# A ring of 41 slots in place of two halves of 20, and the rounds of a block behind the whole next product

## The chip, the cores and the metric

One core of a Trainium2 chip runs the kernel. The metric is the device time of one execution in microseconds, the median of three runs.

## The reference

Two graph layers with a residual and a layer norm each, on x (5120 x 64) with a dense stored adjacency matrix adj (5120 x 5120, float32, 105 MB). The first, cut to what matters:

```
e = concat(c_u * (diag_u * x_u @ W_u) + x_u,  c_i * (diag_i * x_i @ W_i) + x_i)
h = adj @ (adj.T @ e)
x = layernorm(x + layernorm(h) * gamma + beta + x)
```

The second layer drops edges by a softmax threshold. The kernel takes the largest row sum of squares of adj while it reads it; where that stays under a bound, no edge can survive, the message is zero, and the output is layernorm(x), which the first layer's last step can give at once. With these inputs it is so; the branches for surviving edges (`message_pe` and the others) are built and not taken.

## The kernel before, in words

adj is read once, in 10 blocks of 512 columns. A block is 40 tiles of 128 rows (`T` = 40), and two tiles are a unit: 128 x 1024 float32, 512 KB, one load into one slot of 4 KB a partition (`SLOT` = 1024). There are 200 units. `slot_of(v)` puts even blocks into slots 20 to 39 and odd blocks into 0 to 19 (`SLOT_FIRST`, line 44).

For each block c there are two products. The first, adj_c.T @ e, takes the units as they come (`multiply_unit`, matmul on line 1455, 8 TensorE instructions a unit) and sums all 20 in one PSUM bank (`block_bank`). VectorE turns the finished sum in 32 x 32 squares (`turn_half`, 1268), and ScalarE and GpSimd spread it over `col_sum` (`keep_cols`, 1157 and 1079), which has two buffers, for even and odd blocks. The second product, adj_c @ that sum, needs the units transposed: VectorE turns each unit in its slot (`turn_unit`, 1259) once TensorE has used it and ScalarE has scanned it. It runs in rounds of 10, 14 and 16 tiles (`PARTS`, line 47), each in one half of PSUM (`round_banks`, four banks, lower or upper by `upper_banks`), with 128 TensorE instructions a round whatever its size (`multiply_round`, 1475). VectorE adds each round to `h_sum` (`add_round`, 1279, and 1277 for block 0).

A slot is free for the unit two blocks later when the round that reads it is done: SyncE, which issues all loads in order of units (1028), waits for `round_done` of that round (1027). ScalarE scans each unit as it lands (`scan`, 1144 to 1149: squares into one of two scratch tiles, with an accumulator read), waiting for the scan two before, which used the same scratch.

The order of TensorE is written out by hand (1516 to 1541). Block 0's rounds lie between the units of block 1 and the first two of block 2 (`AHEAD`). From then on, with c from 1 to 8: 16 units of block c + 1, round 0 of block c, 4 units of block c + 1, rounds 1 and 2 of block c. At the end block 9's first two rounds (12 and 12 tiles) come before the last round of block 8, and the norm's steps (`close_tiles`, 1490) lie between the rest. VectorE has an order to match (1293 to 1328, then 1367 on).

Slots that are not yet or no longer in use hold other things: x, its transposed pairs and the small weights before block 1 is loaded (so SyncE waits for `e_made`, 1023), x once more at the end (`X_SLOT`, 126, in slots of block 8). `center_t` and `center_g` are small tiles for gamma, used once by the matmul on line 1523.

Of the kernel before, what the change touches and what calls it, by code (L numbers as in the profile page):

```python
# [7 lines left out]
def adjacency_layers_kernel(nc, x, adj, w_ui, scales, gamma, beta,  # L8
# [13 lines left out]
    P = 128  # L22
# [20 lines left out]
    SLOTS = 40  # L43
    SLOT_FIRST = [20 if c % 2 == 0 else 0 for c in range(NB)]
    assert sum(WIDTHS) == N and max(WIDTHS) == CH

    PARTS = [((0, 10), (10, 14), (24, 16))] * (NB - 1)
    PARTS += [((0, 12), (12, 12), (24, 8), (32, 8))]

# [9 lines left out]

    AHEAD = 2  # L60
# [37 lines left out]
    with ctx:  # L98
# [27 lines left out]
        X_SLOT = 20  # L126
# [21 lines left out]
        scratch = [sb(f"scratch{k}", [P, SLOT], bf16) for k in range(2)]  # L148
# [3 lines left out]
        center_t = sb("center_t", [D, P])  # L152
        center_g = sb("center_g", [D, D])
# [7 lines left out]
        inv_d = sb("inv_d", [P, TPG])  # L161
        neg_inv_d = sb("neg_inv_d", [P, TPG])
        eps_tile = sb("eps_tile", [P, TPG])


        piece_at = [N * i for i in range(4)] + [ln_at + N * i for i in range(4)]
        piece = [pooled[:, a:a + N] for a in piece_at]
        assert 4 * N <= x_at and piece_at[-1] + N <= POOLED
# [33 lines left out]
        diagonal = carve(P)  # L202
        node_a, node_b, node_c = carve(T), carve(T), carve(T)
# [151 lines left out]
        def slot_of(v):  # L355
            c, i = place_of_unit(v)
            return SLOT_FIRST[c] + i

# [7 lines left out]
        def banks_of_block(c):  # L366

            return c % 2 == 0

        def upper_banks(g):  # L370

            c = place_of_round(g)[0]
            if c == NB - 1:
                return banks_of_block(NB - 2) == (g != LAST)
            return banks_of_block(c) == (c == NB - 2 or g < ROUNDS_AT[c + 1] - 1)
# [32 lines left out]
        def turned_of(g):  # L410

            c, first, nt = place_of_round(g)
            w = WIDTHS[c]
            at = SLOT * SLOT_FIRST[c] + w * first
            return pooled[:, at:at + w * nt].rearrange("p (t b r) -> p t b r", b=w // 32, t=nt)
# [577 lines left out]
        def message_pool(pool):  # L993
# [10 lines left out]
            pool.wait_ge(gate, (ROUNDS * STAGES + 1) * SHARERS)  # L1004
            with pool.Fori(0, GROUPS) as g:
                step = Steps(pool, g * STEPS1)
                layer_norm(pool, step, ln_h, g * SUMS1, ln_out, (g + 1) * 16)
# [4 lines left out]
        def _(sp):  # L1012
            for k in range(LGROUPS):
                sp.dma_start(x_first[:, group_tiles(k), :], tile_rows(x, GT * k, GT)).then_inc(x_loaded[k], 16)  # L1014
            for v in range(UNITS):
                c, i = place_of_unit(v)
                ut, c0 = UNIT_TILES[c], COL_FIRST[c]
                if v == UNIT_FIRST[1]:
                    sp.dma_start(gamma_sb[:, :], gamma).then_inc(norm_in, 16)  # L1019
                    sp.dma_start(beta_sb[:, :], beta.partition_broadcast(P)).then_inc(norm_in, 16)  # L1020

                    assert SLOT_FIRST[1] == 0 and SETUP_SLOTS <= UPB[1]
                    sp.wait_ge(e_made, LGROUPS)
# [28 lines left out]
        def _(pool):  # L1052
            for tile, value in ((ident, 0.0), (center, 0.0), (minus_half, -0.5), (inv_d, 1.0 / D),
                                (neg_inv_d, -1.0 / D), (eps_tile, LN_EPS)):
                nc.gpsimd.memset(tile[:, :], value).then_inc(cleared, 1)
            pool.wait_ge(cleared, 6)
# [79 lines left out]
        def _(act):  # L1136
# [7 lines left out]
            def scan(v):  # L1144
                wait_loaded(act, v)
                if v >= 2:
                    act.wait_ge(unit_scanned, v - 1)
                nc.scalar.activation(scratch[v % 2][:, :], slots[slot_of(v)], ACT.Square,  # L1148
                                     accum_out=square_sum[:, v:v + 1]).then_inc(unit_scanned, 1)
# [67 lines left out]
        def _(dve):  # L1217
# [92 lines left out]
            for v in range(UNIT_FIRST[1] + 18, UNIT_FIRST[2] + AHEAD):  # L1310
                turn_unit(v)
            add_round(2)


            for c in range(1, NB - 1):
                first = UNIT_FIRST[c + 1]
                for v in range(first + AHEAD if c == 1 else first, first + 13):
                    turn_unit(v)
                add_round(ROUNDS_AT[c])
                turn_unit(first + 13)  # L1320
                turn_half(c + 1)
                if c == NB - 2:
                    break
                for v in range(first + 14, first + 19):
                    turn_unit(v)
                add_round(ROUNDS_AT[c] + 1)
                turn_unit(first + 19)
                add_round(ROUNDS_AT[c] + 2)

# [90 lines left out]
        def _(pe):  # L1420
# [21 lines left out]
            def multiply_unit(v):  # L1442
# [4 lines left out]
                if i == 0 and c >= 2:  # L1447
                    pe.wait_ge(halves_turned_b, c - 1)
                    same = before_in_banks(ROUNDS_AT[c - 1], banks_of_block(c))
                    pe.wait_ge(round_added, same[-1] + 1)  # L1450
# [8 lines left out]
            def multiply_round(g):  # L1459
# [7 lines left out]
                pe.wait_ge(halves_turned_b, c + 1 if banks_of_block(c) == upper_banks(g) else min(c + 2, NB))  # L1467
                if g == 2:
                    pe.wait_ge(center_kept, 1)
# [54 lines left out]
            for v in range(UNIT_FIRST[1] + 12, UNIT_FIRST[2] + AHEAD):  # L1524
# [3 lines left out]


            for c in range(1, NB - 1):  # L1530
                first = UNIT_FIRST[c + 1]
                for v in range(first + AHEAD if c == 1 else first, first + 16):
                    multiply_unit(v)
                multiply_round(ROUNDS_AT[c])
                for v in range(first + 16, first + 20):
                    multiply_unit(v)
                multiply_round(ROUNDS_AT[c] + 1)
                if c < NB - 2:
                    multiply_round(ROUNDS_AT[c] + 2)
# [52 lines left out]
```

## Time and profile before

| | us |
|---|---|
| median of 3 runs (lowest, highest) | 398.53 (398.12, 398.65) |
| the profiled execution | 398.46 |
| its span, first to last instruction | 396.70 |
| TensorE busy in it | 379.2 (96%) |
| VectorE, ScalarE, GpSimd busy | 317.0, 267.5, 63.9 |
| read from HBM | 107.60 MB |

Times in views are from the start of the span. A row of a timeline gives the start, the busy time of the instructions merged in it, the engine and line, what is written from what, how many, and in brackets the idle time just before with what ended it. TensorE's instructions overlap, and their ends are modelled, so a row's length can reach a little over the start of the next.

### The profile page before, as it was taken

What the parts mean: (1) busy time and instruction counts of PE and PEld (TensorE: products, weight loads), DVE (VectorE), ACT (ScalarE), POOL (GpSimd) and SP (SyncE); (2) the same over time, 40 slices, a digit from 0 to 9 for tenths busy, and PEclk for the clock granted to TensorE, in tenths of its full rate; (3) what the DMA queues carried; (4) which work ended last, traced back from release to release, by engine and by line L of the source; (5) the groups of instructions that cost most, each with busy time, mean ns of one, the idle gap of its engine ahead of it and who ended that gap; (6) DMA issues with size and microseconds to landing.
All of it is one profiled execution on the core that took longest, in us unless ns stands there. A gap on an engine that the chain in (4) does not pass through costs nothing.

```text
span 396.7 us, 13295 instructions
## 1 busy us (share of the span) xinstructions
PE 379.2 (96%) x5762; PEld 220.4 (56%) x5762; DVE 317.0 (80%) x306; ACT 267.5 (67%) x515; POOL 63.9 (16%) x125
## 2 busy tenths in 40 slices
PE   8987999999999999999999999999999999999980
PEld 7743556465456546545654664565466456555770
DVE  1699799797788869787976979697698869795674
ACT  2596995996878577587857768685876868501133
POOL 2000300300200300030030003003000300276375
PEclk9999999999999999999999999999999999999996
DMA  8999999894798789579877967996895799300012
GB/s 286 389 387 380 386 386 387 314 388 156 267 377 296 268 311 386 198 268 391 310 264 252 388 222 270 393 339 204 311 387 192 270 393 368 141 3 2 24 35 85
DMA packets 56991, 109.83 MB, mean 277 GB/s; under 512 B 3808, under 2 KB 4576, under 8 KB 56928
## 3 DMA queue, kind: packets, MB, share of 16 engines
q1 hardware_dynamic: 56640, 108.84, 75.9%
q8 instruction: 47, 0.77, 0.8%
q10 hardware_dynamic: 288, 0.09, 0.1%
q14 instruction: 16, 0.13, 0.1%
HBM read 107.60 MB, written 1.31 MB: 275 GB/s over the span
## 4 chain that ended last, share of the span: by engine, by line
PE 85%; SPq 8%; DMA 3%; DVE 1%; POOL 1%; issue 1%; POOLq 0%; ACT 0%; DVEq 0%
PE quad L1475 44%; PE quad L1455 39%; SPq L1028 6%; DMA pooled<-in_adj 3%; PE quad L1490 2%; SPq L1019 1%; DVE pooled L1279 1%; POOL pooled L1107 1%; SPq L1014 1%; POOLq L98 0%; POOL pooled L1102 0%; DVE pooled L1346 0%; DVE pooled L1355 0%; SPq L1020 0%; DVE pooled L1332 0%
## 5 line engine op out<-in xcount | busy, mean ns | idle before, releaser
L1259 DVE STREAM_TRANSPOSE pooled<-pooled 128x1024 f32<-128x1024 f32 x200 | 229.8, 1208 | 7.9 <-ACT scratch L1148 7.9
L1148 ACT ACTIVATE scratch<-pooled 128x1024 bf16<-128x1024 f32 x200 | 210.0, 1051 | 36.1 <-DMA pooled<-in_adj 34.5
L1455 PE MATMUL quad<-pooled,rows_in 128*64 128x256 f32 x1600 | 180.7, 381 | 4.0 <-DMA pooled<-in_adj 4.0
L1475 PE MATMUL quad<-pooled,col_sum 32*64 32x320 f32 (+4 forms) x3968 | 177.5, 507 | 0.6 <-issue 0.2
L1455 PEld LDWEIGHTS quad<-pooled,rows_in 128*64 128x64 f32 x1600 | 111.8, 137 | 74.5 <-issue 12.5
L1475 PEld LDWEIGHTS quad<-pooled,col_sum 32*64 32x64 f32 x3968 | 88.1, 132 | 82.7 <-issue 63.7
L1279 DVE TENSOR_TENSOR pooled<-pooled,quad 128x1280 f32<-128x1280 f32 (+5 forms) x29 | 52.4, 1808 | 43.4 <-PE quad L1475 43.3
L1079 POOL COPY col_sum<-col_half 32x256 f32<-32x256 f32 x80 | 31.6, 394 | 312.4 <-DVE col_half L1268 309.5
L1157 ACT COPY col_sum<-col_half 32x256 f32<-32x256 f32 x80 | 32.3, 403 | 42.5 <-DVE col_half L1268 41.7
L1148 ACT ACTIVATION_READ_ACCUMULATOR scratch<-pooled 128x1 f32 x200 | 37.4, 187 | 0.0
L1178 ACT ACTIVATE pooled<-quad 128x256 f32<-128x256 f32 (+2 forms) x7 | 3.3, 476 | 25.2 <-PE quad L1490 25.2
L1490 PE MATMUL quad<-center,pooled 128*128 128x128 f32 x80 | 10.2, 281 | 1.6 <-DVE pooled L1279 0.9
L1490 PEld LDWEIGHTS quad<-center,pooled 128*128 128x128 f32 x80 | 9.3, 191 | 4.0 <-issue 2.7
L1268 DVE STREAM_TRANSPOSE col_half<-quad 128x256 f32<-128x256 f32 x10 | 4.4, 441 | 7.2 <-PE quad L1455 7.2
L1107 POOL TENSOR_TENSOR pooled<-pooled,minus_half 128x4 f32<-128x4 f32 (+2 forms) x7 | 8.9, 1277 | 7.5 <-DVE pooled L1355 7.4
L1186 ACT ACTIVATE pooled<-pooled 128x256 f32<-128x256 f32 (+2 forms) x7 | 3.5, 507 | 9.6 <-DVE pooled L1350 7.7
L1102 POOL TENSOR_TENSOR pooled<-pooled,minus_half 128x4 f32<-128x4 f32 (+2 forms) x7 | 8.9, 1282 | 4.7 <-DVE pooled L1332 4.6
L1142 ACT COPY pooled<-quad 128x512 f32<-128x512 f32 x5 | 2.8, 587 | 9.8 <-PE quad L1428 9.8
L1232 DVE TENSOR_TENSOR rows_in<-quad,pooled 128x256 f32<-128x256 f32 x10 | 3.7, 411 | 3.6 <-PE quad L1438 3.4
L1097 POOL TENSOR_TENSOR pooled<-pooled,beta_sb 128x512 f32<-128x512 f32 x5 | 6.4, 1277 | 0.4
L1277 DVE COPY pooled<-quad 128x1280 f32<-128x1280 f32 (+2 forms) x3 | 5.8, 1922 | 0.8 <-PE quad L1475 0.8
L1438 PE MATMUL quad<-pooled 64*128 64x64 f32 x80 | 5.5, 278 | 0.3 <-ACT pooled L1142 0.3
(48 smaller groups left out, 60.1 us busy)
## 6 DMA issues: line engine op xcount, KB each, us to landing
pooled<-in_adj SPq DMA_DIRECT2D x200, 512.0 KB, 9.2
pooled<-in_x SPq DMA_DIRECT2D x5, 256.0 KB, 3.7
pooled<-in_x SPq DMA_DIRECT2D x1, 768.0 KB, 5.1
pooled<-in_x SPq DMA_DIRECT2D x1, 512.0 KB, 3.5
out<-pooled SPq DMA_DIRECT2D x2, 256.0 KB, 2.5
out<-pooled SPq DMA_DIRECT2D x2, 192.0 KB, 3.0
out<-pooled SPq DMA_DIRECT2D x3, 128.0 KB, 2.0
pooled<-in_w_ui ACTq DMA_DIRECT2D x1, 64.0 KB, 3.3
```

Of the source, the lines that this page charges most:

```text
L1028: sp.dma_start(slots[slot_of(v)].rearrange("p (t k) -> p t k", t=ut), tile_rows(adj, ut * i, ut)[:, :, c0:c0 + WIDTHS[c]]).then_inc(unit_l ...
L1079: kept = nc.gpsimd.tensor_copy(spread_to(c, a, 1, f), spread_from(c, 1, f))
L1097: nc.gpsimd.tensor_tensor(xk, xk, beta_sb[:, :].unsqueeze(1).to_broadcast([P, GT, D]), ALU.add).then_inc(x_steps, 1)
L1102: nc.gpsimd.tensor_tensor(rstd[:, norm_tiles(k)], var[:, norm_tiles(k)], minus_half[:, 0:norm_size(k)], ALU.pow).then_inc(rstd_made, 1)
L1107: nc.gpsimd.tensor_tensor(scale[:, norm_tiles(k)], y_var[:, norm_tiles(k)], minus_half[:, 0:norm_size(k)], ALU.pow).then_inc(scale_made, 1)
L1148: nc.scalar.activation(scratch[v % 2][:, :], slots[slot_of(v)], ACT.Square, accum_out=square_sum[:, v:v + 1]).then_inc(unit_scanned, 1)
L1157: kept = act.copy(spread_to(c, a, 0, f), spread_from(c, 0, f))
L1259: nc.vector.transpose(tiles, tiles).then_inc(unit_turned, 1)
L1279: nc.vector.tensor_tensor(to, to, share, ALU.add).then_inc(round_added, 1)
L1455: mm = pe.matmul(block_bank(c)[half(h), 0:w // 2], rows_in[:, t, :], slots[slot_of(v)][:, at:at + w // 2], start=(t == 0), stop=(t == T - 1))
L1475: mm = pe.matmul(round_banks(g)[a][half(b % 2), 0:w].rearrange("p (t r) -> p t r", r=32), col_sum[c % 2][quadrant(a), b, :], to[quadrant(a ...
L1490: mm = pe.matmul(nat_of(k)[:, i, :], h_sum[:, P * (first + i):P * (first + i) + P], center[:, :], start=True, stop=True)
```

## The change

The two halves become one ring of 41 slots: unit v of the whole sequence sits in slot (9 + v) mod 41, so a unit takes the slot of the unit before it two blocks earlier. Three blocks get other sizes of rounds, so that no round crosses the ring's end (blocks 3, 5 and 7 with first rounds of 10, 12 and 14 tiles). For the blocks 1 to 7 TensorE does all 20 units of the next block and then the three rounds in a row; VectorE's order follows. The first products of all blocks but 0 use the lower banks; the rounds of a block use upper, lower, upper, and those of blocks 0 and 8 only upper ones. ScalarE's two scratch tiles become one, so a scan waits for the scan just before it, `center_t` and `center_g` move into `h_sum` (VectorE waits for `gamma_turned` before round 2 of block 0 is added), and three constants move into the part for surviving edges. The diff, cut to its core:

```diff
@@ -40,12 +40,17 @@
-    SLOTS = 40
-    SLOT_FIRST = [20 if c % 2 == 0 else 0 for c in range(NB)]
+    SLOTS = 41
+    SLOT_FIRST = [(9 + UNIT_FIRST[c]) % SLOTS for c in range(NB)]
...
     PARTS = [((0, 10), (10, 14), (24, 16))] * (NB - 1)
+    PARTS[3] = ((0, 10), (10, 16), (26, 14))
+    PARTS[5] = ((0, 12), (12, 16), (28, 12))
+    PARTS[7] = ((0, 14), (14, 16), (30, 10))
     PARTS += [((0, 12), (12, 12), (24, 8), (32, 8))]
...
-    AHEAD = 2
...
-        X_SLOT = 20
+        X_SLOT = 5
...
-        scratch = [sb(f"scratch{k}", [P, SLOT], bf16) for k in range(2)]
+        scratch = sb("scratch", [P, SLOT], bf16)
...
-        center_t = sb("center_t", [D, P])
-        center_g = sb("center_g", [D, D])
+
+        center_t = h_sum[0:D, N - P:N]
+        center_g = h_sum[0:D, N - P - D:N - P]
...
-            return SLOT_FIRST[c] + i
+            return (SLOT_FIRST[c] + i) % SLOTS
...
-            return c % 2 == 0
+            return c == 0
 
         def upper_banks(g):
...
             c = place_of_round(g)[0]
-            if c == NB - 1:
-                return banks_of_block(NB - 2) == (g != LAST)
-            return banks_of_block(c) == (c == NB - 2 or g < ROUNDS_AT[c + 1] - 1)
+            if c in (0, NB - 2):
+                return True
+            return g != (LAST if c == NB - 1 else ROUNDS_AT[c] + 1)
...
-
-                    assert SLOT_FIRST[1] == 0 and SETUP_SLOTS <= UPB[1]
+                if v < UNIT_FIRST[2] and slot_of(v) == 0:
+
+                    assert c == 1 and i + SETUP_SLOTS <= UPB[1]
                     sp.wait_ge(e_made, LGROUPS)
...
-            for tile, value in ((ident, 0.0), (center, 0.0), (minus_half, -0.5), (inv_d, 1.0 / D),
-                                (neg_inv_d, -1.0 / D), (eps_tile, LN_EPS)):
+            for tile, value in ((ident, 0.0), (center, 0.0), (minus_half, -0.5)):
                 nc.gpsimd.memset(tile[:, :], value).then_inc(cleared, 1)
-            pool.wait_ge(cleared, 6)
+            pool.wait_ge(cleared, 3)
...
-                if v >= 2:
-                    act.wait_ge(unit_scanned, v - 1)
-                nc.scalar.activation(scratch[v % 2][:, :], slots[slot_of(v)], ACT.Square,
+                if v:
+                    act.wait_ge(unit_scanned, v)
+                nc.scalar.activation(scratch[:, :], slots[slot_of(v)], ACT.Square,
                                      accum_out=square_sum[:, v:v + 1]).then_inc(unit_scanned, 1)
...
-            for v in range(UNIT_FIRST[1] + 18, UNIT_FIRST[2] + AHEAD):
+            for v in range(UNIT_FIRST[1] + 18, UNIT_FIRST[2]):
                 turn_unit(v)
+            dve.wait_ge(gamma_turned, 1)
             add_round(2)
 
 
-            for c in range(1, NB - 1):
+            for c in range(1, NB - 2):
                 first = UNIT_FIRST[c + 1]
-                for v in range(first + AHEAD if c == 1 else first, first + 13):
+                for v in range(first, first + 14):
+                    turn_unit(v)
+                turn_half(c + 1)
+                for v in range(first + 14, first + 18):
                     turn_unit(v)
                 add_round(ROUNDS_AT[c])
-                turn_unit(first + 13)
-                turn_half(c + 1)
-                if c == NB - 2:
-                    break
-                for v in range(first + 14, first + 19):
+                for v in range(first + 18, first + 20):
                     turn_unit(v)
                 add_round(ROUNDS_AT[c] + 1)
-                turn_unit(first + 19)
                 add_round(ROUNDS_AT[c] + 2)
+
+
+            for v in range(UNIT_FIRST[NB - 1], UNITS - 7):
+                turn_unit(v)
+            add_round(ROUNDS_AT[NB - 2])
+            turn_unit(UNITS - 7)
+            turn_half(NB - 1)
...
                 if i == 0 and c >= 2:
-                    pe.wait_ge(halves_turned_b, c - 1)
+
+                    pe.wait_ge(halves_turned_b, c)
                     same = before_in_banks(ROUNDS_AT[c - 1], banks_of_block(c))
-                    pe.wait_ge(round_added, same[-1] + 1)
+                    if same:
+                        pe.wait_ge(round_added, same[-1] + 1)
...
-                pe.wait_ge(halves_turned_b, c + 1 if banks_of_block(c) == upper_banks(g) else min(c + 2, NB))
-                if g == 2:
+                pe.wait_ge(halves_turned_b, 1 if upper_banks(g) else min(c + 2, NB))
+                if g == ROUNDS_AT[1] + 1:
                     pe.wait_ge(center_kept, 1)
...
-            for v in range(UNIT_FIRST[1] + 12, UNIT_FIRST[2] + AHEAD):
+            for v in range(UNIT_FIRST[1] + 12, UNIT_FIRST[2]):
                 multiply_unit(v)
             multiply_round(2)
 
 
-
-            for c in range(1, NB - 1):
-                first = UNIT_FIRST[c + 1]
-                for v in range(first + AHEAD if c == 1 else first, first + 16):
+            for c in range(1, NB - 2):
+                for v in range(UNIT_FIRST[c + 1], UNIT_FIRST[c + 2]):
                     multiply_unit(v)
-                multiply_round(ROUNDS_AT[c])
-                for v in range(first + 16, first + 20):
-                    multiply_unit(v)
-                multiply_round(ROUNDS_AT[c] + 1)
-                if c < NB - 2:
-                    multiply_round(ROUNDS_AT[c] + 2)
+                for g in range(ROUNDS_AT[c], ROUNDS_AT[c + 1]):
+                    multiply_round(g)
+
+
+            for v in range(UNIT_FIRST[NB - 1], UNITS - 4):
+                multiply_unit(v)
+            multiply_round(ROUNDS_AT[NB - 2])
+            for v in range(UNITS - 4, UNITS):
+                multiply_unit(v)
+            multiply_round(ROUNDS_AT[NB - 2] + 1)
             multiply_round(LAST)
             multiply_round(LAST + 1)
             close_tiles(0)
```

## Rows read from the trace of the kernel before

**Rows 1.** the page: busy time by engine, and the chain by engine

```profile
PE 379.2 (96%) x5762; PEld 220.4 (56%) x5762; DVE 317.0 (80%) x306; ACT 267.5 (67%) x515; POOL 63.9 (16%) x125
...
PE 85%; SPq 8%; DMA 3%; DVE 1%; POOL 1%; issue 1%; POOLq 0%; ACT 0%; DVEq 0%
```

**Rows 2.** timeline of TensorE: start us, busy us, instruction

```profile
42.83 1.08 PE L1455 MATMUL quad<-pooled,rows_in 128*64 128x256 f32 x8 [0.27 <-DMA pooled<-in_adj]
...
61.27 8.85 PE L1455 MATMUL quad<-pooled,rows_in 128*64 128x256 f32 x80
...
70.33 7.13 PE L1475 MATMUL quad<-pooled,col_sum 32*64 32x512 f32 x128 [0.20 <-issue]
...
110.79 14.03 PE L1455 MATMUL quad<-pooled,rows_in 128*64 128x256 f32 x128
...
124.75 4.56 PE L1475 MATMUL quad<-pooled,col_sum 32*64 32x320 f32 x128
...
129.24 3.67 PE L1455 MATMUL quad<-pooled,rows_in 128*64 128x256 f32 x32
...
132.85 13.13 PE L1475 MATMUL quad<-pooled,col_sum 32*64 32x448 f32 x256
...
145.91 14.03 PE L1455 MATMUL quad<-pooled,rows_in 128*64 128x256 f32 x128
...
343.61 16.59 PE L1475 MATMUL quad<-pooled,col_sum 32*64 32x448 f32 x384
...
371.86 3.71 PE L1475 MATMUL quad<-pooled,col_sum 32*64 32x256 f32 x128
```

**Rows 3.** timeline of SyncE's queue, loads of line 1028

```profile
129.41 0.37 SPq L1028 DMA_DIRECT2D pooled<-in_adj  x1
...
139.22 0.37 SPq L1028 DMA_DIRECT2D pooled<-in_adj  x1
...
314.85 0.37 SPq L1028 DMA_DIRECT2D pooled<-in_adj  x1
```

**Rows 4.** timeline of ScalarE, scans that waited for their load

```profile
143.03 1.06 ACT L1148 ACTIVATE scratch<-pooled 128x1024 bf16<-128x1024 f32 x1 [0.94 <-DMA pooled<-in_adj]
...
161.87 1.06 ACT L1148 ACTIVATE scratch<-pooled 128x1024 bf16<-128x1024 f32 x1 [0.16 <-DMA pooled<-in_adj]
...
337.57 1.06 ACT L1148 ACTIVATE scratch<-pooled 128x1024 bf16<-128x1024 f32 x1 [0.15 <-DMA pooled<-in_adj]
```

**Rows 5.** stretches: busy us (count) by engine, granted clock, DMA share, GB/s

```profile
135.00:136.00 1.00, 1.00 (x32) 0.45 (x24) 1.00 (x2) 0.96 (x4) 0.92 (x3) 1.00 0.94 291
...
141.50:160.50 19.00, 19.00 (x238) 11.14 (x229) 15.31 (x13) 14.39 (x26) 0.00 (x0) 1.00 1.05 389
...
273.00:276.00 3.00, 3.00 (x60) 1.30 (x64) 2.53 (x3) 2.00 (x5) 1.85 (x5) 1.00 0.90 281
```

**Rows 6.** timelines of ScalarE, GpSimd and VectorE in the first 53 us

```profile
16.53 1.06 ACT L1148 ACTIVATE scratch<-pooled 128x1024 bf16<-128x1024 f32 x1
...
17.49 0.19 ACT L1148 ACTIVATION_READ_ACCUMULATOR scratch<-pooled 128x1 f32 x1
...
17.58 1.04 ACT L1148 ACTIVATE scratch<-pooled 128x1024 bf16<-128x1024 f32 x1
...
40.21 3.31 ACT L1157 COPY col_sum<-col_half 32x256 f32<-32x256 f32 x8 [3.13 <-DVE col_half L1268]
...
1.48 0.29 POOL L1057 TENSOR_SCALAR_AFFINE_SELECT ident<-ident 128x128 f32<-128x128 f32 x1 [0.25 <-POOL eps_tile L1055]
...
52.23 0.15 DVE L1248 TENSOR_SCALAR beta_sum<-beta_sum 128x1 f32<-128x1 f32 x1
...
52.42 0.26 DVE L1250 TENSOR_SCALAR beta_sb<-beta_sb,beta_sum 128x64 f32<-128x64 f32 x1
```

**Rows 7.** timeline of VectorE in the block from 145.91

```profile
146.09 2.29 DVE L1279 TENSOR_TENSOR pooled<-pooled,quad 128x2048 f32<-128x2048 f32 x1 [3.69 <-PE quad L1475]
...
148.29 14.76 DVE L1259 STREAM_TRANSPOSE pooled<-pooled 128x1024 f32<-128x1024 f32 x13
```

More of the change, by code:

```diff
@@ L41, in adjacency_layers_kernel @@
     UNITS = UNIT_FIRST[NB]
-    SLOTS = 40
-    SLOT_FIRST = [20 if c % 2 == 0 else 0 for c in range(NB)]
+    SLOTS = 41
+    SLOT_FIRST = [(9 + UNIT_FIRST[c]) % SLOTS for c in range(NB)]
     assert sum(WIDTHS) == N and max(WIDTHS) == CH
     PARTS = [((0, 10), (10, 14), (24, 16))] * (NB - 1)
+    PARTS[3] = ((0, 10), (10, 16), (26, 14))
+    PARTS[5] = ((0, 12), (12, 16), (28, 12))
+    PARTS[7] = ((0, 14), (14, 16), (30, 10))
     PARTS += [((0, 12), (12, 12), (24, 8), (32, 8))]
+    assert all((SLOT_FIRST[c] + t // UNIT_TILES[c]) % SLOTS + nt // UNIT_TILES[c] <= SLOTS
+               for c in range(NB) for t, nt in PARTS[c])
     ORDER = [(c,) + part for c in range(NB - 1) for part in PARTS[c]]
@@ L160, in adjacency_layers_kernel @@
         minus_half = sb("minus_half", [P, GT])
[L161 to L166, printed above, removed]
+        piece_at = [0] + [ln_at + N * i for i in range(7)]
         piece = [pooled[:, a:a + N] for a in piece_at]
-        assert 4 * N <= x_at and piece_at[-1] + N <= POOLED
+        assert N <= x_at and piece_at[-1] + N <= POOLED
         ring, turned, carved_from, rest = piece[0:4], piece[4:6], piece[6], piece[7]
@@ L202, in adjacency_layers_kernel @@
         diagonal = carve(P)
+        inv_d, neg_inv_d, eps_tile = carve(TPG), carve(TPG), carve(TPG)
         node_a, node_b, node_c = carve(T), carve(T), carve(T)
@@ L413, in turned_of @@
             w = WIDTHS[c]
-            at = SLOT * SLOT_FIRST[c] + w * first
+            at = SLOT * slot_of(UNIT_FIRST[c] + first // UNIT_TILES[c])
             return pooled[:, at:at + w * nt].rearrange("p (t b r) -> p t b r", b=w // 32, t=nt)
@@ L1004, in message_pool @@
             pool.wait_ge(gate, (ROUNDS * STAGES + 1) * SHARERS)
+            for tile, value in ((inv_d, 1.0 / D), (neg_inv_d, -1.0 / D), (eps_tile, LN_EPS)):
+                nc.gpsimd.memset(tile[:, :], value).then_inc(cleared, 1)
+            pool.wait_ge(cleared, 6)
             with pool.Fori(0, GROUPS) as g:
```

## Prediction

> **What bounds the kernel now.** Read first the page's engine line and its chain. TensorE is busy 96% of the span, and 85% of the chain that ended last is TensorE; transfers hold 3% of it, nearly all in the first 43 us [rows 1]. From 43 to 360 us TensorE is the clock of everything, so the next view is its timeline [rows 2]. One block costs 35.12 us (from 110.79 to 145.91), and it is made of four runs: 16 units of the next first product, round 0, the last 4 units, rounds 1 and 2. The starts follow each other without a gap. So this change can only gain by what TensorE loses when it goes from one kind of work to the other, and can only lose by making TensorE wait.
>
> The switch has a price that the rows give. Unit runs take 8.85 us for 80 instructions and 14.03 for 128: 0.108 us each (0.863 for a unit of 8) and 0.22 once per run. Round runs take 4.56 us for 10 tiles and 13.13 for two rounds with 30 tiles: 0.4285 a tile and 0.27 once. The run of three rounds, 38 tiles, takes 16.59, where 0.4285 x 38 + 0.27 = 16.55: the constant belongs to the run, not to the round. The 8-tile round fits too (3.70 against 3.71). The next run starts 0.07 before the modelled end of the last, so a run costs 0.15 (units) or 0.20 (rounds). Check: 20 x 0.863 + 40 x 0.4285 + 2 x 0.15 + 2 x 0.20 = 35.10, read 35.12 [rows 2].
>
> **What is removed.** In the blocks 1 to 7 the rounds now form one run behind one run of 20 units: 0.35 us less in each of 7 cycles, 2.45. The split of the 40 tiles among three rounds moves, their sum doesn't. Round 2 of block 0 waited 0.20 us for the turned half of block 1, as it shared its banks [rows 2]; it now goes to the upper banks, where nothing is late: 0.20. In all 2.65 us less, if the data are there. Block 0 and the end (16 units, round 0 of block 8, 4 units, the rest) keep their order and are costed at nothing.
>
> **What is moved: the time in which slots come free.** Unit i of a block is loaded into the slot of unit i - 1 two blocks before. Before, round 0 ran in the middle of the next product, and 15 of the 20 loads were let go by rounds 1 and 2. After, unit 0 goes into the spare slot, but units 1 to 19 all wait for round 0, which now starts only when the whole product between is done. The loop of the changed kernel is then: round 0, release, 19 loads, last unit, round 0. I compute both sides from the release.
>
> TensorE's side: SyncE issues 4.66 us after a 10-tile round started (129.41 against 124.75) [rows 2, 3]. The three rounds take 17.14 + 0.20 = 17.34, so the product starts 12.68 after the issue and its unit 19 is wanted 19 x 0.863 = 16.40 later: 29.1 us after the issue.
>
> The loads' side: ScalarE scans each unit as it lands, so its starts that end a wait on DMA are landings. In the stretch that follows the issue at 139.22, the first of 15 units lands at 143.03 (3.81 later), the 14th, the last but one, at 161.87 (22.65 later) [rows 3, 4]. The last such stretch gives 337.57 - 314.85 = 22.72, and the four between lie from 22.5 to 23.05. The queues move 389 GB/s there [rows 5], 1.35 us for a unit of 524,288 bytes; 13 steps would be 17.55, and 18.84 are read, so somewhere 1.29 us are lost in each stretch while the bytes flow at an even rate. After the change unit 19 is the last but one of 20 loads (unit 0 of the next block follows it): 22.7 + 5 x 1.35 = 29.45 us. It comes 0.35 us late, and the restart makes the last unit 1.08 instead of some 0.96 us (42.83 alone, as in the start [rows 2]): 0.45 us a cycle. The cover that hid the loads, 4 us of round 0 in the middle of the product, is gone.
>
> The rule on completion in the Trainium skill (DMA: Bandwidth & Descriptors, section "Why a DMA increments its semaphore by 16 and not by 1") says that a transfer counts as landed only when the slowest of its engines is done; by that, one engine that falls behind delays every later unit though the rate looks whole. The even 389 GB/s beside the lost 1.29 us agrees.
>
> Cycle by cycle: block 2's loads start early enough (slots of block 0 are free by 76 us), no stall. Blocks 3, 4, 5, 6 and 8: 0.45 each, 2.25. Block 7 waits for round 0 of block 5, which now has 12 tiles, so the release is 0.86 later: 1.3. Block 9 waits for a 14-tile round 0 (1.71 later), but its last 4 units run after a round; its unit 15 lands 24.05 after the issue and is wanted 23.9 after it: 0.15. Sum 3.7 us.
>
> One more cost is due to lost slack. The rate sags now and then: 291 GB/s in 135 to 136, 281 in 273 to 276 [rows 5], 0.25 + 0.83 = 1.1 us of transfer lost in the stretches behind round 0, where nobody waited then. Six of seven such stretches now end on the path: 0.9 us (bounds 0 and 2).
>
> **What is hidden.** VectorE: 20 transposes at 1.135 us are 22.7 us of a block, and three round sums are under 2.3 each [rows 7], so some 5 us are free. In the new order 14 transposes end 0.9 us after the product, the half is turned by 1.4, and the lower banks are wanted by round 1 at 4.5; if that cover went, TensorE would wait for the difference. Every unit is turned a whole product before its round. The 8 copies of col_sum on ScalarE and GpSimd (3.3 us) are wanted 17 us later. SyncE: the wait for e_made moves 12 loads down its queue; it is over by then in any case (TensorE can't have used block 0 without e), and the gamma and beta loads stay where they were. GpSimd has three memsets less to wait for before ident, but TensorE is then in its warm-up: 0. The wait for gamma_turned on VectorE holds back add_round(2) alone, which comes 10 us later.
>
> ScalarE's single scratch adds a wait of each scan for the scan before. Now a scan starts every 1.04 us, even 0.10 before the accumulator read of the last ends (17.49 + 0.19 = 17.68, next at 17.58) [rows 6]. No row shows ScalarE waiting for itself. VectorE does it in 0.04 us (0.15 us from 52.23, next at 52.42), GpSimd in 0.25 (idle before 1.48) [rows 6]: 1.19 to 1.40 us a scan. [...] It matters in one place, the start: 19 scans from 16.53 must end before the copies at 40.21, which a spacing up to 1.25 allows; at 1.40 round 0 of block 0 would start up to 2.3 us late. Later ScalarE follows the loads at 1.35 a unit and has time. Cost 0, bounds 0 and 2.3.
>
> **The sum.** The profiled execution took 398.46 us (span 396.70 and 1.76 around it), 0.07 under the median of 398.53. 398.46 - 2.65 + 3.7 + 0.9 = 400.4.
>
> **Rivals.** (1) The loads arrive in time: faster. If the 1.29 us don't recur in a stretch begun by round 0, unit 19 lands 28.15 after the issue, before 29.1, block 7 is just met, and 2.65 remain: 395.8. For it: the loss is not seen in every step, and the stretches behind round 0 can't be read (ScalarE is busy copying). Against: it is there in all six stretches (the first and the last of them: [rows 3, 4]). It decides where a landing is under 29.1. The Trainium skill (same page, section "Anatomy of one DMA", a fit for GpSimd's queue) gives 2.0 us plus bytes over 436 GB/s. An estimate by it puts the 19 units at 24.8 us, that is, on the side of this rival at 395.8; the 389 GB/s and the 3.81 us to the first landing speak against both of its figures here. (2) A draw: the lateness is there, but 0.1 to 0.3 a cycle, and gives back what the runs gained: 397.7 to 399.3, likeliest 398.6. (3) The loss grows with the length of the stretch: 1.29 x 18/13 = 1.79, 0.5 more in 7 cycles: 403.9. (4) The single scratch is slow at the start, 1.30 or more a scan: 1 to 2.3 us on top, around 402, or 397 with rival 1. (5) A run of merged rounds doesn't lose its constants, since the banks change between them: then 2.45 is not gained; against it speaks the 38-tile run [rows 2].
>
> **Chances.** The forecast (stalls of 0.35 us a cycle or more, to 402) 0.45; rival 1 0.28; rival 2 0.15; rivals 3 to 5 together 0.12. What a measurement of this kernel can tell from no change is about 0.2%, 0.8 us. Faster than 397.7: 0.30 (rival 1 and the edge of 2). Within: 0.15. Slower than 399.3: 0.55. The range must reach to rival 1, as it holds more than 2 in 10: 395.7 below, and 402.8 above, which leaves out most of rival 3. The forecast alone would have 399.3 to 402.
>
> **What the next profile would show.** In TensorE's timeline runs of 160 unit instructions, each ahead of one run of 384 round instructions. Right: a block takes about 35.2 us, not 34.8; the unit run is cut near its end by a wait on the loads; that wait is longest in block 7, at 36; DMA idles some 4 us a block, all of it ahead of round 0's end; round 2 of block 0 has no wait. Wrong: unit runs of 17.5 us with no wait on DMA (rival 1), scans further apart than 1.25 us in the first 40 us (rival 4), or 0.2 us between rounds of one run (rival 5). The forecast stands or falls with one number, the landing of unit 19 after the issue behind round 0: each 0.1 us of it moves the sum by 0.7.

## The result and the profile after

| | before | after |
|---|---|---|
| median of 6 runs (lowest, highest) | 398.54 us (397.60, 399.28) | 401.94 us (400.82, 402.55) |
| ratio, with its 95% interval | | 1.008 (1.0064 to 1.0096) |
| profiled execution, its span | 398.46, 396.70 | 400.82, 399.0 |

The change costs 3.4 us in the medians. The page of the changed kernel, busy time by engine and the chain by engine, to hold against [rows 1]:

```profile
PE 378.5 (95%) x5762; PEld 218.8 (55%) x5762; DVE 316.2 (79%) x306; ACT 276.2 (69%) x515; POOL 63.8 (16%) x122
...
PE 64%; DMA 17%; SPq 14%; DVE 1%; issue 1%; POOL 1%; POOLq 0%; ACT 0%; DVEq 0%
```

TensorE is busy for the same time, but the chain has moved: TensorE's share fell from 85% to 64%, transfers rose from 3% to 17% and SyncE's queue from 8% to 14%. The loads have come onto the path. TensorE's timeline shows where (start us, busy us, instruction, how many, idle before with what ended it); the lines from 60.48 on answer to [rows 2]:

```profile
60.48 7.13 PE L1468 MATMUL quad<-pooled,rows_in 128*64 128x256 f32 x64
67.53 7.12 PE L1488 MATMUL quad<-pooled,col_sum 32*64 32x512 f32 x128
...
109.38 15.81 PE L1468 MATMUL quad<-pooled,rows_in 128*64 128x256 f32 x144
125.56 1.08 PE L1468 MATMUL quad<-pooled,rows_in 128*64 128x256 f32 x8 [0.38 <-DMA pooled<-in_adj]
126.84 1.08 PE L1468 MATMUL quad<-pooled,rows_in 128*64 128x256 f32 x8 [0.20 <-DMA pooled<-in_adj]
127.86 17.44 PE L1488 MATMUL quad<-pooled,col_sum 32*64 32x320 f32 x384
145.23 17.69 PE L1468 MATMUL quad<-pooled,rows_in 128*64 128x256 f32 x160
162.85 17.44 PE L1488 MATMUL quad<-pooled,col_sum 32*64 32x320 f32 x384
...
197.30 1.08 PE L1468 MATMUL quad<-pooled,rows_in 128*64 128x256 f32 x8 [0.21 <-DMA pooled<-in_adj]
...
233.47 17.80 PE L1488 MATMUL quad<-pooled,col_sum 32*64 32x384 f32 x384
251.21 14.96 PE L1468 MATMUL quad<-pooled,rows_in 128*64 128x256 f32 x136
266.43 1.08 PE L1468 MATMUL quad<-pooled,rows_in 128*64 128x256 f32 x8 [0.27 <-DMA pooled<-in_adj]
268.88 1.08 PE L1468 MATMUL quad<-pooled,rows_in 128*64 128x256 f32 x8 [1.37 <-DMA pooled<-in_adj]
270.17 1.08 PE L1468 MATMUL quad<-pooled,rows_in 128*64 128x256 f32 x8 [0.21 <-DMA pooled<-in_adj]
271.19 17.44 PE L1488 MATMUL quad<-pooled,col_sum 32*64 32x320 f32 x384
```

The new order is there: 160 unit instructions, 384 round instructions, with no constant lost between rounds of a run (17.44 us for 40 tiles; 0.4285 x 40 + 0.27 = 17.41). One run of rounds, from 233.47, took 17.80; the 0.36 us more are no wait on a load. Round 2 of block 0 (67.53) has lost its wait of 0.20. But unit runs end in single units of 8 instructions, each behind a wait on a load, as at the start of the kernel. Where no wait is printed, as in 145.23, the run is still longer (17.69) than the 17.49 that it takes with data at hand.

The stretches from one first product to the next answer to the 35.12 us between 110.79 and 145.91 in [rows 2] (columns: stretch, its length, busy us and count of TensorE, weight loads, VectorE, ScalarE, GpSimd, granted clock, DMA share, GB/s):

```profile
109.38:145.23 35.85, 35.28 (x553) 19.59 (x545) 28.71 (x24) 27.06 (x50) 3.16 (x8) 1.00 0.83 302
145.23:180.22 34.99, 34.99 (x552) 19.74 (x544) 28.86 (x24) 26.29 (x50) 3.16 (x8) 1.00 0.83 298
180.22:215.69 35.47, 35.24 (x553) 19.67 (x545) 28.45 (x24) 25.90 (x48) 3.16 (x8) 1.00 0.83 301
215.69:251.21 35.52, 35.37 (x553) 19.88 (x545) 29.24 (x24) 25.35 (x48) 3.16 (x8) 1.00 0.79 284
251.21:288.56 37.35, 35.51 (x546) 19.48 (x544) 28.18 (x24) 27.11 (x51) 3.15 (x8) 1.00 0.82 297
288.56:323.68 35.12, 35.01 (x552) 19.75 (x544) 29.51 (x24) 24.95 (x47) 3.15 (x8) 1.00 0.78 282
```

The granted clock is 1.00 (the 2.4 GHz level) and the work the same in each of the six, yet they take 35.0 to 37.35 us.

This profiled execution is the fastest of the six. From the unit run behind gamma (60.48, before 61.27) to the 38-tile run (345.78, before 343.61) it took 2.96 us more; the part ahead of it, where the first loads set the pace, was 0.79 shorter, and what follows 0.13 longer.

### The profile page after: what moved, and what is told of

It is laid out like the page before. It is cut to its first block, busy times and chain, and to the rows that moved or that the text cites. A ratio compares the mean times of both kernels' runs of the same rounds, so it can differ in the third digit from the quotient of the medians.

```text
span 399.0 us, 13294 instructions
## 1 busy us (share of the span) xinstructions
PE 378.5 (95%) x5762; PEld 218.8 (55%) x5762; DVE 316.2 (79%) x306; ACT 276.2 (69%) x515; POOL 63.8 (16%) x122
## 4 chain that ended last, share of the span: by engine, by line
PE 64%; DMA 17%; SPq 14%; DVE 1%; issue 1%; POOL 1%; POOLq 0%; ACT 0%; DVEq 0%
PE quad L1488 44%; PE quad L1468 18%; DMA pooled<-in_adj 17%; SPq L1034 13%; PE quad L1503 2%; SPq L1024 1%; DVE pooled L1284 1%; POOL pooled L1112 1%; SPq L1019 1%; POOLq L101 0%; POOL pooled L1107 0%; DVE pooled L1357 0%; DVE pooled L1366 0%; SPq L1025 0%; DVE pooled L1343 0%
## 5 line engine op out<-in xcount | busy, mean ns | idle before, releaser
L1488 PE MATMUL quad<-pooled,col_sum 32*64 32x512 f32 (+4 forms) x3968 | 176.1, 506 | 0.3 <-DVE pooled L1284 0.2
L1284 DVE TENSOR_TENSOR pooled<-pooled,quad 128x2048 f32<-128x2048 f32 (+5 forms) x29 | 52.2, 1802 | 50.6 <-PE quad L1488 50.5
```

The lines of the kernel that those rows point to most:

```text
L1284: nc.vector.tensor_tensor(to, to, share, ALU.add).then_inc(round_added, 1)
L1488: mm = pe.matmul(round_banks(g)[a][half(b % 2), 0:w].rearrange("p (t r) -> p t r", r=32), col_sum[c % 2][quadrant(a), b, :], to[quadrant(a ...
```

## Experiments

The theory: TensorE gains 2.65 us, and all the loss is loads that are late because 19 of 20 wait for a round 0 that starts only behind the whole product. Rivals: the scratch, the ring with its other sizes of rounds, or the merged runs themselves cost time.

**One scratch alone.**

```diff
-        scratch = [sb(f"scratch{k}", [P, SLOT], bf16) for k in range(2)]
+        scratch = sb("scratch", [P, SLOT], bf16)
...
-                if v >= 2:
-                    act.wait_ge(unit_scanned, v - 1)
+                if v:
+                    act.wait_ge(unit_scanned, v)
```

> The kernel before with one part of the change alone: ScalarE's two scratch tiles become one, so a scan waits for the scan just before it. Theory (late loads): scans stand 1.24 us apart where they followed each other at 1.04, nobody waits for them, and the time stays at 398.5 us (398.2 to 398.9). Rival (the single scratch is part of the loss): 399.3 to 402. In this kernel VectorE turns a unit sooner after its scan than in the changed one, so this is the harder case for the scratch.

Measured 398.74 us, ratio 1.0004 (0.999 to 1.0019). The scans of its trace (ScalarE, around the copies of col_sum) stand 1.24 us apart; [rows 6] had 1.04:

```profile
37.80 1.06 ACT L1148 ACTIVATE scratch<-pooled 128x1024 bf16<-128x1024 f32 x1
...
39.04 1.06 ACT L1148 ACTIVATE scratch<-pooled 128x1024 bf16<-128x1024 f32 x1
...
40.17 3.31 ACT L1157 COPY col_sum<-col_half 32x256 f32<-32x256 f32 x8
```

The last scan before the copies ends just in time for them (they start at 40.17; 40.21 before). So the scratch costs nothing, by a small margin: beyond 1.25 us a scan it would have held up round 0 of block 0, by the prediction's count.

**Loads that can't be late, in either order.**

```diff
+                lt = 1 if c in FEW else ut
-                sp.dma_start(slots[slot_of(v)].rearrange("p (t k) -> p t k", t=ut),
-                             tile_rows(adj, ut * i, ut)[:, :, c0:c0 + WIDTHS[c]]).then_inc(...)
+                sp.dma_start(slots[slot_of(v)].rearrange("p (t k) -> p t k", t=ut)[:, 0:lt, :],
+                             tile_rows(adj, ut * i, lt)[:, :, c0:c0 + WIDTHS[c]]).then_inc(...)
```

with `FEW = range(3, NB)`, put into the kernel before:

> The kernel before, but from block 3 on only the first tile of each unit is loaded (256 KB in place of 512 KB; the second tile keeps what was in the slot). Part of the computation is left out: the output isn't the reference's. Everything else, with all waits, stays. Loads were hidden already from 43 us on, so every theory expects 398.5 us (398.0 to 398.8); it is the partner of the next kernel.

and into the changed one:

> The changed kernel with the same half loads from block 3 on (part of the computation is left out, the output isn't the reference's). No load can be late. Theory (TensorE gains 0.35 us for each pair of runs merged and 0.2 at round 2 of block 0, and all the loss is late loads): 2.65 us under the kernel before, 395.9 (395.4 to 396.4), TensorE without a gap in any unit run. Rival (the new order doesn't gain, or the scratch or the banks cost): 398 or more.

Measured 398.58 us (0.9997, 0.9985 to 1.0009) and 395.46 us (0.9917, 0.99 to 0.9934). TensorE's timeline of the second:

```profile
60.76 7.13 PE L1470 MATMUL quad<-pooled,rows_in 128*64 128x256 f32 x64
...
109.66 17.49 PE L1470 MATMUL quad<-pooled,rows_in 128*64 128x256 f32 x160
127.07 17.44 PE L1490 MATMUL quad<-pooled,col_sum 32*64 32x320 f32 x384
144.45 17.49 PE L1470 MATMUL quad<-pooled,rows_in 128*64 128x256 f32 x160
...
340.46 16.59 PE L1490 MATMUL quad<-pooled,col_sum 32*64 32x448 f32 x384
```

Every cycle takes 34.79 us, 0.33 less than 35.12, and from 60.76 to 340.46 it is 279.70 where the kernel before had 282.34: 2.64 less. So the order brings what the runs' constants promised, and the loss of the changed kernel is gone with half of its load traffic. The further 0.4 lies ahead of 60 us, where the kept profiles of all kernels differ by a microsecond in any case (the run behind gamma starts between 60.48 and 61.59).

**The order undone, the ring kept.** In blocks 1 to 7 round 0 stands behind 16 units again (`SPLIT = range(1, 8)`), with banks and VectorE's order to match:

```diff
+                if c in SPLIT:
+                    for v in range(UNIT_FIRST[c + 1], UNIT_FIRST[c + 2] - 4):
+                        multiply_unit(v)
+                    multiply_round(ROUNDS_AT[c])
+                    for v in range(UNIT_FIRST[c + 2] - 4, UNIT_FIRST[c + 2]):
+                        multiply_unit(v)
+                    multiply_round(ROUNDS_AT[c] + 1)
+                    multiply_round(ROUNDS_AT[c] + 2)
+                    continue
```

> The changed kernel with the order of work undone: ring of 41 slots, single scratch and the changed sizes of rounds stay, but in all blocks 1 to 7 round 0 stands behind 16 units again. Theory (the order alone makes the loads late; ring, sizes and scratch cost nothing): 398.3 (397.9 to 398.7). Rival (the ring or the other round sizes are part of the loss): 400 or more.

Measured 397.89 us, 0.9989 (0.9979 to 0.9999). The interval lies just under 1: ring, scratch and the sizes of the rounds cost nothing, and together (with the wait of 0.20 us at round 2 of block 0 gone) they bring some 0.4 us. The loss belongs to the order.

**One more load behind the release.** The changed order with the old 40 slots:

```diff
-    SLOTS = 41
-    SLOT_FIRST = [(9 + UNIT_FIRST[c]) % SLOTS for c in range(NB)]
+    SLOTS = 40
+    SLOT_FIRST = [20 if c % 2 == 0 else 0 for c in range(NB)]
```

and without the three lines on `PARTS[3]`, `PARTS[5]` and `PARTS[7]` (the tiles that lie in the slots before and after use move back with it). Beside it the changed kernel once more.

> The changed kernel without the spare slot: 40 slots in two halves as before, rounds of 10, 14 and 16 tiles in every block, the order of work of the changed kernel. Unit 0 of a block now waits for round 0 too, so the last unit is the 20th load behind the release, not the 19th. Theory (late loads): 1.35 us more in each of six cycles, 8.1; block 7's release comes 0.86 earlier than in the changed kernel: 401.9 + 7.2 = 409. Rival (the wait isn't a matter of the number of loads behind the release): 402.

> The changed kernel once more, beside the next ones on the same chip: 401.9 us (400.8 to 402.6), and its own loss of 1 to 3 us in the unit runs of blocks 3 to 8.

Measured 408.67 us (1.0257, 1.0231 to 1.0284) against 402.05 (1.0087, 1.0065 to 1.0108): 6.6 us more, where 7.2 were expected. In its trace the unit runs end in more waits on loads, and one of 1.18 us where a transfer came late:

```profile
110.04 14.17 PE L1465 MATMUL quad<-pooled,rows_in 128*64 128x256 f32 x128
124.49 1.08 PE L1465 MATMUL quad<-pooled,rows_in 128*64 128x256 f32 x8 [0.27 <-DMA pooled<-in_adj]
126.75 1.08 PE L1465 MATMUL quad<-pooled,rows_in 128*64 128x256 f32 x8 [1.18 <-DMA pooled<-in_adj]
128.04 1.08 PE L1465 MATMUL quad<-pooled,rows_in 128*64 128x256 f32 x8 [0.21 <-DMA pooled<-in_adj]
```

**An earlier and a later release.** First the rounds of blocks 1, 2, 4 and 6 with a first round of 8 tiles, then 12 tiles in blocks 1, 2, 3, 4 and 6:

```diff
+    for c in (1, 2, 4, 6):
+        PARTS[c] = ((0, 8), (8, 16), (24, 16))
```

```diff
-    PARTS[3] = ((0, 10), (10, 16), (26, 14))
+    for c in (1, 2, 3, 4, 6):
+        PARTS[c] = ((0, 12), (12, 12), (24, 16)) if c == 1 else ((0, 12), (12, 14), (26, 14))
```

> The changed kernel, but the rounds of blocks 1, 2, 4 and 6 have 8, 16 and 16 tiles in place of 10, 14 and 16, so SyncE is let go 0.86 us earlier in these four; their loads are those of blocks 3, 4, 6 and 8. Theory (the loop is release, 19 loads, last unit): the lateness of these four cycles in the profile of the changed kernel was 1.10, 0.24, 0.77 and 0.37 us over a full-speed cycle; each gets back up to 0.86, in all 2.2 us: 399.7 from 401.9. Rival (the size of the first round doesn't matter): 401.9.

> The changed kernel with first rounds of 12 tiles in blocks 1, 2, 3, 4 and 6 (12, 12, 16 in block 1, else 12, 14, 14), so the release comes 0.86 us later in five cycles. Smaller first rounds (8 tiles) had cost 3 us, with the DMA rate falling to 66 to 86 GB/s for a microsecond behind the first four loads. Theory (each load's place behind the release counts, and the queue must not run dry before the next round is done; six loads last 8.1 us, the next release comes after 6): 5 x 0.86 = 4.3 more than the changed kernel, 406.3 (405.3 to 407). Rival (the stalls come from the queue running dry behind small first rounds, so larger ones cure them): under 402.

Measured 404.98 us (1.0167, 1.0127 to 1.0207) and 404.79 us (1.0155, 1.014 to 1.0171). The first is a miss: 3 us more than the changed kernel, not 2.2 less. Its DMA rate behind an 8-tile round (block 4's, released at 204.2) shows what happened (columns as above, GB/s last):

```profile
203.50:211.00 7.50, 7.50 (x160) 3.36 (x152) 5.33 (x5) 3.57 (x7) 0.87 (x3) 1.00 0.77 263
211.00:212.00 1.00, 1.00 (x24) 0.36 (x16) 0.95 (x1) 0.83 (x3) 0.00 (x0) 1.00 0.43 143
212.00:213.00 1.00, 1.00 (x32) 0.47 (x24) 1.00 (x1) 0.97 (x2) 0.00 (x0) 1.00 0.72 147
218.00:230.00 12.00, 12.00 (x114) 8.02 (x112) 12.00 (x10) 9.51 (x18) 0.00 (x0) 1.00 1.04 386
```

Four loads let go by a round of 8 tiles last 3.81 + 3 x 1.35 = 7.9 us from the issue; the next release comes 16 x 0.4285 = 6.9 us after it, and its bytes need another 1 to 2 us to flow, so the queues run half empty for two microseconds (143 and 147 GB/s). At 386 GB/s the bytes missed in them are 1.25 us of transfer, more than the 0.86 us that the earlier release brought. The changed kernel has a smaller hole of this kind itself: block 3's first round of 10 tiles is followed by one of 16, and behind it the rate falls to 244 and 344 GB/s for two microseconds (175.5 to 177.5). With 12 tiles there is no such hole, and the kernel takes 2.7 us more than the changed one. That is outside the range expected, but far from the rival's 402: a later release costs time, though a cycle's loss isn't the release alone. Of the three first rounds tried, 10 tiles followed by 14 (6.0 us, against 5 loads that last 9.2) is the best.

**Four rounds, the first of 6 tiles.** Blocks 2 to 7 get rounds of 6, 10, 12 and 12 tiles or the like (block 1: 8, 16, 16), with banks that alternate:

```diff
-    PARTS[3] = ((0, 10), (10, 16), (26, 14))
-    PARTS[5] = ((0, 12), (12, 16), (28, 12))
-    PARTS[7] = ((0, 14), (14, 16), (30, 10))
+    PARTS[1] = ((0, 8), (8, 16), (24, 16))
+    for c in (2, 4, 6):
+        PARTS[c] = ((0, 6), (6, 10), (16, 12), (28, 12))
+    PARTS[3] = ((0, 6), (6, 10), (16, 10), (26, 14))
+    PARTS[5] = ((0, 6), (6, 10), (16, 12), (28, 12))
+    PARTS[7] = ((0, 6), (6, 10), (16, 14), (30, 10))
```

> The changed kernel with its stall cured: four rounds in the blocks 2 to 7, the first of 6 tiles (block 1 keeps three, 8, 16 and 16), banks alternating so that the last round never holds up the next product. The release comes 1.71 us earlier than with 10 tiles, 2.57 earlier in block 5, and a further round in one run costs TensorE nothing. Theory: no stall but some 0.3 us in block 3, and the 2.65 us are kept: 396.2 (395.8 to 397), faster than both kernels. Rival (rounds cost TensorE 0.27 us each even in one run, or VectorE's fourth sum comes late): 398 or more.

Measured 413.97 us (1.0386, 1.0364 to 1.0407), a miss by 18 us. The loads are on time, as expected: from block 4 on the unit runs take 17.49 us. It is the round runs that have holes:

```profile
149.75 17.49 PE L1479 MATMUL quad<-pooled,rows_in 128*64 128x256 f32 x160
167.17 9.31 PE L1499 MATMUL quad<-pooled,col_sum 32*64 32x192 f32 x319
177.65 5.42 PE L1499 MATMUL quad<-pooled,col_sum 32*64 32x320 f32 x127 [1.18 <-issue]
184.24 3.91 PE L1499 MATMUL quad<-pooled,col_sum 32*64 32x448 f32 x66 [1.17 <-issue]
```

The idle times end in "issue": TensorE waited for nothing that the profile shows, in the middle of a round, where the code has no wait. The stretch from 145 to 148 in windows (TensorE busy 1.12 of 3 us, the DMA engines full, 399 GB/s):

```profile
145.00:148.00 3.00, 1.12 (x30) 0.56 (x12) 0.00 (x0) 1.27 (x3) 0.00 (x0) 1.00 1.05 399
```

A round takes 128 matmul and 128 weight-load records whatever its size, so a fourth round puts 1,024 records in place of 768 into 17.4 us. Either the instructions came late or VectorE's sums did (VectorE is idle in this stretch, 0.00 us busy, which speaks against the second), and the same kernel with half loads was to tell. Its further edit is the one shown above for half loads.

> The four-round kernel (e_four, 414 us, whose unit runs had no wait but whose round runs had gaps of 0.3 to 2.2 us in mid-round with nothing to wait for), with half loads from block 3 on: only the first tile of each unit is loaded, so part of the computation is left out and the output isn't the reference's. Theory A (TensorE ran out of instructions: 512 matmul and 512 weight-load records in 17.4 us, fetched over DMA engines that are full of loads): with the queues half empty the gaps vanish, 395.5 as in the changed kernel with half loads. Theory B (the instructions can't come faster whatever the loads do, or a wait on VectorE's sums is behind it): the gaps stay, 408 or more.

Measured 396.82 us (0.9948, 0.9936 to 0.9961). Most round runs are whole, two are 0.8 and 0.7 us too long:

```profile
127.69 17.48 PE L1501 MATMUL quad<-pooled,col_sum 32*64 32x192 f32 x512
...
162.52 18.31 PE L1501 MATMUL quad<-pooled,col_sum 32*64 32x192 f32 x512
...
198.18 18.14 PE L1501 MATMUL quad<-pooled,col_sum 32*64 32x192 f32 x512
```

Of 18.5 us over the changed kernel with half loads, 1.4 are left (some 1.7 of the 18.5 were a late load in block 3, whose release comes from an 8-tile round followed by one of 16). VectorE's work and all waits are the same in both, so the holes come from load traffic meeting many TensorE instructions. The Trainium skill (Runtime: NRT & Kernel Launch, section "Instruction fetch mechanics") says that instructions are refilled in blocks of 16 KiB (256 instructions) by the sequencer's own DMA queue, and calls that cost mostly hidden. The traces bear out the blocks: the instruction queue moved 47 packets in the changed kernel and 53 here, six more for six more rounds of 256 records each, and each packet has 16,384 bytes.

That it is the fetch can be read from the four-round kernel's trace. Counted in order, matmuls and weight loads together, its holes stand at TensorE's records 4033, 5058, 5313, 6338, 6593, 9154, 9409 and 10689, always a multiple of 256 apart, give or take one. And each ends 1.3 to 1.55 us after a packet of the instruction queue is through. For the hole that ends at 148.27 it is the packet from 145.76 to 146.80, the only one between 139.2 and 148.3 (DMA queues in the window 145.7 to 146.9: packets, MB, share):

```profile
q8 instruction: 1, 0.02, 5.4%
```

TensorE had come to the block before at 140.59. That packet started 5.2 us later, with the engines full of loads (366 GB/s); the block of 256 records was used up after 5.5 us, and the next stood ready only after 7.7. Where hardly anything is being loaded in this trace (under 30 GB/s), a packet starts 0.5 to 1.3 us after TensorE comes to the block before its own; ahead of the eight holes it starts 3.2 to 5.2 us after it. What decides among the queues inside the DMA engines isn't shown. But in these holes TensorE was short of instructions, not of data.

**Merge only where the loads can follow.** If a merged cycle makes loads late only when the next product is merged too, every other cycle may be merged (`SPLIT = (2, 4, 6)`), and with block 5's late release left out as well three (`SPLIT = (2, 4, 5, 6)`):

> The ring of 41 slots and the single scratch, but only every other cycle merged: the rounds of blocks 1, 3, 5 and 7 stand as one run behind the whole next product, those of 2, 4 and 6 as before (round 0 behind 16 units). Banks follow. Theory (a merged cycle makes loads late only where the next product but one is merged too, as its unit 19 is wanted 4.5 us later when a round 0 lies in it): no stall but 0.1 to 0.5 in block 9; four merges at 0.35 and the 0.2 at round 2 of block 0 are kept: 1.6 less than before, 397.0 (396.6 to 397.5). Rival (any merge costs what it brings): 398.5 or more.

> As the kernel with every other cycle merged, but block 5's rounds are split again, so merged runs stand behind the products 2, 4 and 8 alone. In the alternating kernel's profile 2.3 us were lost in the two cycles after block 5's 12-tile first round, 0.83 of it as a gap in mid-round without any wait. Theory (the loss there came from the late release behind a 12-tile first round in a merged cycle): three merges at 0.35 and the 0.2 are kept, 1.25 us under the kernel before, 397.3 (396.9 to 397.8). Rival (merged cycles lose what they bring wherever they stand): 398.2 to 398.6.

Measured 398.24 us (0.9991, 0.9973 to 1.0008) and 397.41 us (0.9972, 0.9957 to 0.9987). The first is a miss: 1.2 us over the forecast, and no change that could be told. In its profile (399.83 us, so one of its slowest executions) the cycles with the merged rounds of blocks 1 and 3 were whole (34.79 us), and the time was lost behind the merged rounds of block 5:

```profile
250.47 13.29 PE L1491 MATMUL quad<-pooled,rows_in 128*64 128x256 f32 x120
264.03 1.08 PE L1491 MATMUL quad<-pooled,rows_in 128*64 128x256 f32 x8 [0.27 <-DMA pooled<-in_adj]
265.04 4.54 PE L1511 MATMUL quad<-pooled,col_sum 32*64 32x320 f32 x121
270.41 0.76 PE L1511 MATMUL quad<-pooled,col_sum 32*64 32x320 f32 x7 [0.83 <-issue]
```

The 16th unit of block 7 was late behind a release by a 12-tile round, and there is a hole of 0.83 us in mid-round as in the four-round kernel: at record 7618, which is a multiple of 256 away from the others, and 1.30 us behind an instruction packet. With that cycle split again 397.3 was expected and 397.41 came. Its interval lies wholly under 1, by 0.28% at the middle: faster than the kernel before, and by some 4.5 us than the changed one. Of the 0.28%, the ring with no cycle merged has 0.11, and the two intervals overlap. That the three merges bring the rest is shown by the profile and not by the medians: its merged cycles take 34.79 us, 0.33 less than before, with no wait in them.

## Why the prediction was right, and which term was too small

**The gain on TensorE (2.65 us).** Right: 2.64 where the loads don't interfere, a cycle of 34.79 against 34.77 by the sum. Rival 5 (no constant saved between banks) is out. The wait at round 2 of block 0 went.

**The landing of unit 19, the number on which the forecast stood or fell.** It was put 29.45 us behind the issue that round 0 of the block two before lets go. SyncE's issues in the changed kernel answer to [rows 3]:

```profile
96.67 0.37 SPq L1034 DMA_DIRECT2D pooled<-in_adj  x1
```

```profile
238.99 1.50 SPq L1034 DMA_DIRECT2D pooled<-in_adj  x2
```

Unit 19 of block 3 started at 126.84, 30.17 later; that of block 7 at 270.17, 31.18 later. For blocks 4, 5, 6 and 8 the same reading gives 29.3, 29.8, 29.5 and 29.4. Four of the six are within 0.35 us of the estimate, none started before 29.1, and rival 1 is out. What sets the loop is release, 19 loads, last unit, round 0, as predicted.

**The stalls (3.7 us) and the sags (0.9).** Right in kind, 1.0 too small together. Over 34.79 the six cycles took 1.06, 0.20, 0.68, 0.73, 2.56 and 0.33 more, and the last 22.10 against 22.06: 5.6 in all. The step that was mis-sized is the even lateness: 0.45 us a cycle, 1.3 in block 7, and 0.9 for sags on top. Block 7 alone cost 2.56. ScalarE's scans show two losses in it (idle before, ended by the load):

```profile
242.81 1.06 ACT L1153 ACTIVATE scratch<-pooled 128x1024 bf16<-128x1024 f32 x1 [4.01 <-DMA pooled<-in_adj]
...
245.86 1.06 ACT L1153 ACTIVATE scratch<-pooled 128x1024 bf16<-128x1024 f32 x1 [1.90 <-DMA pooled<-in_adj]
...
247.18 1.06 ACT L1153 ACTIVATE scratch<-pooled 128x1024 bf16<-128x1024 f32 x1 [0.17 <-DMA pooled<-in_adj]
...
266.41 1.06 ACT L1153 ACTIVATE scratch<-pooled 128x1024 bf16<-128x1024 f32 x1 [0.21 <-DMA pooled<-in_adj]
...
268.86 1.06 ACT L1153 ACTIVATE scratch<-pooled 128x1024 bf16<-128x1024 f32 x1 [1.30 <-DMA pooled<-in_adj]
```

From 242.81 to 245.86 the rate had sagged (295 GB/s from 242 to 245, where 386 is read from 246 to 264). Around the landing at 268.86 it hadn't, as far as can be told (376 from 265 to 268; behind that it falls, since the stretch's last loads are running out), yet the transfer came 1.1 us late. A step of this kind is in each of the stretches of [rows 4], once; a stretch of 19 loads has room for a second. That was rival 3's mechanism, and it showed in one cycle of six in this execution.

The sum made the other cost, the sags, from two of seven stretches. And 0.37 of block 6's 0.73 isn't a load's at all: it is the longer run of rounds from 233.47, a cost that the prediction doesn't have. In the profile the sum is 398.46 - 2.65 + 5.6 = 401.4, less 0.8 at the start, plus 0.13 at the end: 400.8, where 400.4 was forecast. This execution was the fastest of six. The medians differ by 3.4 us, so the usual loss is nearer 3.4 + 2.65 = 6.05, 1.45 more than the 4.6 that were put.

**Where the loss falls, and luck.** The second profile of the changed kernel (the one beside the 40 slots, 402.23 us) tells what one profile can't. Its six cycles lost 1.50, 0.09, 1.91, 0.39, 2.29 and 0.19 us, and the last stretch 0.15: 6.5 in all. Unit 19 of block 7 came 30.56 us behind its issue at 241.05:

```profile
271.61 1.08 PE L1468 MATMUL quad<-pooled,rows_in 128*64 128x256 f32 x8 [0.20 <-DMA pooled<-in_adj]
```

In both profiles the loads of blocks 3, 5 and 7 cost most of it (4.30 of 5.6 and 5.70 of 6.5), and those of blocks 4, 6 and 8 hardly anything. So the extra isn't just chance from run to run, and only one of the ten cycles put at 0.45 is near it (0.39). Part of it has a place: in both, the rate sags 3 to 6 us behind the issues for blocks 3 and 7 (295 GB/s from 242 to 245 in the first profile, 248 and 238 from 244 to 246 in the second), and behind block 5's there is the hole that a round of 16 tiles leaves (down to 244 GB/s in the first, 211 in the second). Why the rate sags behind two of the releases and not behind the rest is open. That terms of 0.45, partly too large and partly far too small, add up to 4.6 of 5.6 or 6.5 is in part luck; the mechanism, the sign and the number on which the sum was built aren't.

**Block 9** was put at 0.15 and cost 0.04. **What was called hidden** stayed hidden: VectorE, the copies, SyncE's moved wait. **The scratch** was put between 1.19 and 1.40 us a scan, with a limit of 1.25; it is 1.24. The verdict (0) was right, with 0.01 us a scan to spare.

**Draw or growth.** Rival 2 needed 0.1 to 0.3 us a cycle. One or two of six cycles were near it (0.20 and 0.33, in the second profile 0.09 and 0.19), the sum far above it.

## What to carry to other kernels

Where a stage runs without a gap, moving a step later in its order also moves every buffer that this step frees; work out the time from the release to the last load wanted, with its startup, the count behind the release and one lagging transfer, before counting the gain. A split run that looks wasteful (0.35 us a block) may be what pays for the transfers, and then half of the merges keeps more than all of them. Smaller first pieces release sooner, but that helps only if what they release lasts until the next release. And compare two profiles of the same kernel before calling a lost microsecond an accident: what comes back in the same place has a cause.

## What the runs showed of the hardware

- TensorE stood still for up to 2.15 us in mid-round with nothing to wait for, when 1,024 of its records fell into 17.4 us beside full load queues (366 GB/s ahead of that hole, 399 in it); with half of the loads the loss fell from 18.5 us to 1.4. The holes stand multiples of 256 records apart, and each ends 1.3 to 1.55 us after a 16,384-byte packet of the instruction queue. Such a packet starts 0.5 to 1.3 us after TensorE comes to the block before when next to nothing is loaded, and 3.2 to 5.2 us after it ahead of the holes.
- A stretch of back-to-back loads loses 1.1 to 1.3 us in one step while the bytes flow on evenly (389 GB/s from 141.5 to 160.5 in the kernel before), once in 15 loads; in one of the six stretches of 19 loads a second step of 1.1 us came.
- Loads behind a release last 3.8 us for the first and 1.35 us for each further one; when the next release came 6.9 us after one of four loads, the rate fell to 143 GB/s.
- A scan of ScalarE that waits for the one just before it takes 0.20 us longer (1.04 to 1.24).
